# Linear attention in a two-layer decoder kernel: VectorE's feature map of the first step moves ahead of measuring the next batch, TensorE's turning of the next rows behind two other turnings

## The reference, cut to what matters

```python
def _phi(x):
    return jax.nn.elu(x) + 1.0
qkv = jnp.einsum('bld,ed->ble', x, w_qkv)
q, k, v = (_phi(qkv[0]), _phi(qkv[1]), qkv[2])
def step(carry, inp):
    S = S + k_t[..., :, None] * v_t[..., None, :]
    z = z + k_t
    num = jnp.einsum('bhde,bhd->bhe', S, q_t)
    den = jnp.maximum(jnp.sum(z * q_t, axis=-1, keepdims=True), EPS)
    return ((S, z), num / den)
return jnp.einsum('bld,ed->ble', out, w_out)
```

## Time and profile before

| | |
|---|---|
| median of three runs | 3820.56 us |
| profiled execution, its own time | 3820.83 us |
| its span | 3819.1 us |
| TensorE busy (matmul) | 3505.7 us, 92% |
| VectorE busy | 2801.9 us, 73% |
| ScalarE busy | 2065.1 us, 54% |
| GpSimd busy | 395.4 us, 10% |
| mean granted TensorE clock | 0.971 of full speed |

### The profile page before, as it was taken

The page is one execution under the profiler, slowest core; times in us unless marked ns, Lnnn a source line. Parts: engine busy times, 40 slices in busy tenths (PEclk is TensorE's granted clock), DMA queues, the critical chain, the costliest instruction groups (busy, mean ns, idle before and its releaser), DMA issues. The chain is left out here.

```text
span 3819.1 us, 91322 instructions
## 1 busy us (share of the span) xinstructions
PE 3505.7 (92%) x28322; PEld 2917.3 (76%) x28322; DVE 2801.9 (73%) x8965; ACT 2065.1 (54%) x6485; POOL 395.4 (10%) x582
## 2 busy tenths in 40 slices
PE   6999999899999999339968889999799999999999
PEld 5888888688888888239956656676588888888887
DVE  5666666677777776646658877888788878788786
ACT  5777777677777776325545548888432223222232
POOL 0000000000000000341168302222000000000000
PEclk9999999999999999669989999999899999999999
DMA  3000000010000000542211000000200000000000
GB/s 101 1 0 0 0 0 0 18 51 11 11 11 13 14 11 1 175 137 77 78 55 45 15 17 20 22 22 17 87 26 11 14 8 16 8 11 14 8 14 9
DMA packets 56108, 109.69 MB, mean 29 GB/s; under 512 B 8368, under 2 KB 27184, under 8 KB 55728
## 3 DMA queue, kind: packets, MB, share of 16 engines
q1 hardware_dynamic: 46656, 80.72, 6.7%
q0 software_dynamic: 8464, 26.22, 2.1%
q10 hardware_dynamic: 864, 1.19, 0.1%
HBM read 72.46 MB, written 35.65 MB: 28 GB/s over the span
## 5 line engine op out<-in xcount | busy, mean ns | idle before, releaser
L2255 DVE TENSOR_TENSOR f_zgT<-f_zT,f_ps_g 128x512 fp32r<-128x512 f32 x512 | 327.3, 681 | 14.0 <-PE f_ps_g L2086 9.9
L639 ACT ACTIVATE c_pr<-c_sm,c_nmx 128x256 f32<-128x256 f32 x512 | 254.5, 498 | 147.7 <-DVE c_nmx L485 147.7
L127 PE MATMUL f_ps_out<-f_out_rounded,f_zgT 128*128 128x256 f32 x1024 | 295.3, 288 | 0.0
L128 PE MATMUL f_ps_out<-f_out_rest,f_zgT 128*128 128x256 f32 x1024 | 289.5, 283 | 0.0
L2208 DVE TENSOR_TENSOR f_gv<-f_ps_v,f_gm 128x512 f32<-128x512 f32 x256 | 175.6, 686 | 154.2 <-PE f_ps_v L129 154.1
L129 PE MATMUL f_ps_out<-f_out_rounded,f_zgT 128*128 128x256 f32 x1024 | 288.0, 281 | 0.0
L639 ACT ACTIVATE a_pr<-a_sm,a_nmx 128x128 f32<-128x128 f32 (+1 forms) x512 | 227.1, 445 | 98.1 <-DVE a_nmx L485 98.1
L485 DVE CUSTOM_DVE_ANT_0 a_sm<-a_ps_s,causal 128x128 f32<-128x128 f32 (+1 forms) x512 | 152.5, 354 | 156.8 <-PE a_ps_s L371 156.7
L485 DVE CUSTOM_DVE_ANT_0 c_sm<-c_ps_s,c_mask 128x256 f32<-128x256 f32 x512 | 186.7, 420 | 87.1 <-PE c_ps_s L371 86.7
L127 PE MATMUL f_ps_v<-f_val_rounded,f_xs 128*128 128x512 f32 x512 | 214.8, 419 | 6.7 <-DVE f_gv L2208 6.7
L2337 ACT ACTIVATE f_pr<-f_sm,f_nmx 128x128 f32<-128x128 f32 (+1 forms) x256 | 115.0, 450 | 185.5 <-DVE f_nmx L2228 185.5
(11 more groups left out here) (384 smaller groups left out, 11231.8 us busy)
## 6 DMA issues: line engine op xcount, KB each, us to landing
f_slot_rows<-f_run POOLq DMA_DIRECT2D x1, 9216.0 KB, 34.8
f_rows<-f_slot_rows SPq DMA_DIRECT2D x72, 128.0 KB, 2.0
f_slot_out<-f_y SPq DMA_DIRECT2D x72, 128.0 KB, 1.9
c_ctx_stage<-in_ctxT SPq DMA_DIRECT2D x32, 256.0 KB, 2.8
small<-in_f_w SPq DMA_DIRECT2D x16, 512.0 KB, 3.9
x_sb<-in_x SPq DMA_DIRECT2D x8, 512.0 KB, 8.3
small<-in_c_w SPq DMA_DIRECT2D x8, 512.0 KB, 4.0
c_mask_stage<-in_mask SPq DMA_DIRECT2D x16, 256.0 KB, 3.0
```

The lines of the kernel that those rows point to most:

```text
L127: nc.tensor.matmul(out, sh, mh, start=start, stop=False, **kw)
L128: nc.tensor.matmul(out, sh, ml, start=False, stop=False, **kw)
L639: last = nc.scalar.activation(pr[:, r, i, 0:n], sm[:, j, i, 0:n], ACT.Exp, bias=nmx[:, j, i:i + 1], scale=-1.0, accum_out=sums[:, r, i:i + 1])
L2255: last = nc.vector.tensor_tensor(zgT[:, k % 2, r], zT[:, s % 2, r, :].bitcast(F32).unsqueeze(1).broadcast_to([P, 2, S]), ps_g[:].rearrange ...
```

## The change

TensorE: in the linear attention only, `turn_x` moves in step 3 from the head of the slot to behind `back` and `turn_o`. VectorE: `features` of step 0 moves ahead of the first masking and of `measure`, which itself moves from ahead of `finish` to behind `features`; `features` of step 2 keeps its place, between the first and second masking. In the last batch, which measures nothing, `features` of step 0 still moves ahead of the first masking.

```diff
@@ TensorE
             def slot(b, s):
-                if s == STEPS - 1 and (not isinstance(b, int) or b + 1 < B):
+                if softmax and s == STEPS - 1 and (not isinstance(b, int) or b + 1 < B):
                     turn_x(b + 1)
                 if at := lagged(b, s, 0, STEPS):
                     project(*at)
...
                     turn_o(at[2])
+                if not softmax and s == STEPS - 1 and (not isinstance(b, int) or b + 1 < B):
+                    turn_x(b + 1)
                 two = lagged(b, s, 2, STEPS) if softmax else None
@@ VectorE
                 else:
-                    if s == 0 and (not isinstance(b, int) or b + 1 < B):
-                        measure(b + 1)
                     if ended:
                         finish(*ended)
                     for j in range(J):
+                        if now and s % 2 == 0 and j == s // 2:
+                            features(*now)
+                            if s == 0 and (not isinstance(b, int) or b + 1 < B):
+                                measure(b + 1)
                         if one:
                             keep_past(one[0], one[1], j)
-                        if now and s % 2 == 0 and j == 0:
-                            features(*now)
                     if one:
                         fill_v(*one)
```

## The result

The changed kernel takes 3806.72 us, the median of five runs (3804.79 to 3811.46), against 3820.56 for the kernel before. The ratio is 0.9962 (95% interval 0.9951 to 0.9973): 13.8 us less, where 10.3 were forecast, and inside the range. The profiled execution took 3811.46 us, the longest of the five, for a span of 3809.7 at a mean granted clock of 0.968.

A forecast was written before the change was run, and what follows sets the result against it. The prediction took the linear attention's order of work to bound it: VectorE waits for z's turning back, behind a late feature map. 9.2 us from waits plus 1.1 from batch 0 made 10.3 less, 3810.3 us, range 3804.5 to 3816.5.

The forecast's parts named there:

- The ring: Linear attention batch: feature map, v projection, turning back of z (L1511), finish; VectorE's 9.4 us in 14 waits stem from it.
- Part 1: Step 0's feature map ahead of measuring and first masking: 0.70 us per undisturbed batch, 9.2 us over the stage.
- Part 2: Measuring placed after the feature map in step 0: costs nothing, covered by ScalarE's earlier start.
- Part 3: turn_x behind back and turn_o in step 3: others fill its 0.44 us stall; no gain, no loss.
- Part 4: Batch 0's feature map, 1.8 us late, starts earlier but partly at the lower clock: 1.1 us, between 0 and 1.8.
- Part 5: Last batch, without measuring, waits 1.49 us for the turning back behind the output matmuls: no gain.
- Part 6: Gap of 0.64 us at the loop's top, 12 times: taken as nothing, bounds -1.4 and +1.2 us.
- Beside GpSimd: Disturbed part of the stage, before 2133: 5.1 us for eight waits, mostly as long as undisturbed ones.
- A: GpSimd takes the gain in disturbed batches; six undisturbed ones and batch 0 leave 5.3 us, 3815.3. Chance 0.12.
- B: Gap at the loop's top was measuring's; up to 0.61 us goes 12 times, 7.3 us more, 3803.0. Chance 0.08.
- C: ScalarE's table loads and v copy come 0.3 us later, delaying TensorE's projection: 4 us given back, 3814.3. Chance 0.07.
- D: TensorE's full clock granted one batch later after batch 0: some +15 us against -10, 3825. Chance 0.03.

The follow-up runs named there:

- e6: The change, with step 3's statistics of the finished batch moved between finish and the four maskings: 3840.18 us, ratio 0.999, undisturbed batch 17.62 us.
- e3: The changed kernel with measuring left at the head of step 0, ahead of finish: ratio 1.0005 to the kernel before, undisturbed batch 17.97 us.
- e4: The change with step 0 as finish, measuring, first masking, feature map: ratio 1.0004 to the kernel before, undisturbed batch 18.37 us.
- e1: Kernel before with only turn_x moved, VectorE's order as before: 3848.59 us against 3844.66, ratio 1.0007, undisturbed batch 18.44 us.
- b2: Changed kernel with turn_x in its old place (VectorE's part alone), last job: 3807.89 us against 3822.41, ratio 0.9963, undisturbed batch 17.50 us.
- e2b: VectorE's part of the change alone, turn_x in its old place, run again in the second job: 3837.75 us, ratio 0.9982 to the kernel before.
- b1: The change itself, run again in the last job: 3808.97 us against 3822.41 for the kernel before, ratio 0.9967.
- b7: VectorE's part alone, plus step 3's statistics of the finished batch ahead of the fill, last job: 3805.57 us against 3822.41, ratio 0.9957.
- a1: The change itself, run again in the second job: 3840.99 us against 3844.88 for the kernel before, ratio 0.9991.
- e2: Changed kernel with turn_x in its old place (VectorE's part alone), first run: 3840.12 us against 3844.66, ratio 0.9981, undisturbed batch 17.50 us.
- e5: The change, with step 3's statistics of the finished batch ahead of the fill copies: 3839.11 us, ratio 0.9985 to the kernel before.

## Why the prediction was right, and where its terms were not

The forecast was 3810.3 us with a range of 3804.5 to 3816.5; measured, 3806.72. The ring that it named is the one that bounded the batch: the wait for L1511 that it set out to remove went, and e6 brought it back. That the total is off by only 3.6 us owes something to luck, as the ledger below shows: two terms too large stand against two gains that it didn't have. Its parts, in its order:

- **Part 1, the feature map.** Right in place and nearly in size. It put 0.70 us on the stretch up to step 1's first masking (5.73 us from the batch's start); measured 0.62 (5.81 us). What it said would be late next is what is late next: maskings end at 2203.70 + 1.95 = 2205.65, the next one starts 1.07 us later, against the 1.06 that was taken over from step 3, with 0.17 us of waiting for the scores. The 9.2 us over the stage took the list's whole waits; at 0.62 us in each of 13 batches they would be 8.1.
- **Part 2, measuring.** Nothing lost, as forecast: ScalarE's table load starts 3.06 us behind the batch's first instruction, instead of 2216.14 - 2212.22 = 3.92. But the part was costed by itself, and e3 and e4 show that it can't be: without it the feature map is worth 0.47 us, with it 0.95.
- **Part 3, turn_x.** Right. e1 has the batch of before to 0.01 us, and b2 has the gain without it. In the change step 3 reads

```profile
2211.96 0.44 PE L1511 MATMUL l_ps_t<-ident,l_zT 128*128 128x128 f32 x2 [0.49 <-ACT l_zT L1800]
2212.24 0.60 PE L1521 MATMUL l_ps_t<-ident,l_o_all 128*128 128x128 f32 x4
2212.68 0.60 PE L1428 MATMUL l_ps_p<-ident,l_xn 128*128 128x128 f32 x4
...
2213.62 0.94 PE L1472 MATMUL l_ps_s<-l_qk,l_split 32*128 32x256 f32 x16 [0.34 <-DVE l_wT L1636]
```

  and the scores still wait for the maskings, 0.34 us instead of 0.17. The others did not fill the stall, as the prediction had it: `back` at the head waits 0.49 us for ScalarE's copy of z, where turn_x waited 0.44 us for the feature map. The maskings end last either way, and so nothing came of it in an undisturbed batch; beside ScalarE's stand a loss of some 3 us is not excluded (e1, e2b).
- **Part 4, batch 0.** Forecast 1.1 us, bounds 0 to 1.8. The feature map came at once behind its input (1968.06 + 0.63, then 1968.72), and the maskings of step 1 stand 1.5 us earlier from the stage's start. Little is left at batch 1:

```profile
1976.73 0.82 DVE L1614 COPY l_vp<-l_v_all 128x64 f32<-128x64 f32 x2
...
1985.05 0.17 DVE L1642 TENSOR_SCALAR l_den<-l_ps_t 128x8 f32<-128x8 f32 x1 [0.83 <-PE l_ps_t L1511]
```

  The fill took 0.82 us beside GpSimd instead of 0.38, and `finish`, now first in line, waits 0.83 us where measuring used to fill that time. Batch 1 starts 40.16 us behind the stage's start instead of 40.27, and 39.80 in b1. The term, 0.1 and 0.5 us, lies near its lower bound.
- **Part 5, the last batch.** Right: 1.50 us of waiting where there were 1.49.
- **Part 6, the top of the loop.** The failed term: taken as nothing, measured 0.31 us a batch, 12 times, 3.7 us, outside its bounds of -1.4 to +1.2 (in this profile 10 of the 12 starts show the gap of some 0.33 us, two show none). It is why the undisturbed batch is 17.49 us and not the 17.7 to 17.8 that was named as the sign. Its reason, "two register instructions fewer", was too small by far, and the row that said so was quoted beside it: outside the loop `finish` followed the statistics with no gap. Here a gap that the profile puts down to "issue" at a loop's top belonged in half to the instruction behind it.
- **Beside GpSimd.** Forecast, 5.1 us for eight waits, of which 4.3 us in six lie in batches 2 to 8; measured, 9.5 us in these seven batches (7.4 in b1). Seven times the 0.95 us of an undisturbed batch is 6.7, which leaves 2.8 (0.7 in b1). VectorE is also busy 3.1 us less in them (121.9 before, 118.8 with the change; b1 1.3 less), 1.6 of it in the fill's copies (0.1 in b1), so that meetings with GpSimd cost less, by an amount that differs from execution to execution. The sum of the waits was no upper bound. (The fill of 1.02 us in the earlier trace rows stands in batch 4, the one batch in the loop without the wait, as counted here.)

The ledger for the profile: forecast 9.2 + 1.1 = 10.3; measured in the stage 12.7, of which the loop's top gave 3.7, the batches beside GpSimd 2.8 more than undisturbed ones, and batch 0 0.1, with 1.6 lost to the clock at the end. That leaves 7.7 us for the waits, where 9.2 were forecast.

**The rivals.** A, GpSimd takes the gain, is refuted where ScalarE doesn't stand, and with the opposite sign: a disturbed batch gained 1.35 us (1.05 in b1), an undisturbed one 0.95. In the two jobs where ScalarE does stand the total came out near A's (3.9 us of gain, A had 5.3), but by a wait of ScalarE. The rule of the Trainium skill that was set beside it (SBUF — State Buffer, Who interferes with whom), that the engine that issues first holds the shared port pair for its whole instruction and the other blocks, agrees with pairs of copies that took 0.82 us beside 0.28; the step from it, that the delays stay with the number of GpSimd's instructions, fell: that number was the same, and b7's copies took 275 ns on the mean where b1's took 354. B, the gap was measuring's, was half right: 0.31 of its 0.61 us went, and it shortened the batch only together with the other move (e4 has the shorter gap and 0.07 us of gain). C, ScalarE's chain, didn't come: the copy of v at 2206.99 lets TensorE start the projection at 2207.61 without a wait. D, the clock: counted from the stage's start, full speed came in batch 0 within 0.5 us of the time at which it came before. It fell again at the end of the stage, which D had no place for, at 1.6 us.

## What to carry to other kernels

An engine's order within a slot is worth reading as a ring: find the wait that ends last, name the instruction ahead of it whose input had long been ready, and move that one ahead; the next limit can be forecast from a step that is already in that state. The gains of two moves need not add up: here one gave 0.47 us, the other 0.07, both 0.95, so test them apart and together. Where an instruction with more waits and register work ahead of it goes, behind the loop's top, a short instruction or a long one, is worth a run of its own. And a gain can shrink to a third in another job, if an engine stands there for reasons of its own; compare the undisturbed batch first, then the total.

## What was not expected of the hardware

- ScalarE's stand of 3.1 to 4.1 us (a1, 2000:2120) once in each round of GpSimd's four gathers, in two jobs and not in the other runs, with nothing in the profile that releases it. The stage of the same kernel is 28.5 us longer in the job that has it (a1: 351.1 us, b1: 322.6). The granted clock shows it too: 0.93 and 0.83 in a1's 2040:2090 and 2090:2130, where the first profiles have 1.00. What holds ScalarE stays open.
- TensorE's clock drops from 2.4 to 1.2 GHz in the stage's tail in one execution and not in another of the same kernel (e2 against b2: 1.99 and 3.78 us for the same eight matmuls), with nothing in the program that differs.
- The 0.64 us at the loop's top, against the compare-and-branch of about 108 ns that the Trainium skill states (Advanced Engine Details and Errata, Control Flow Timing): no run here shows the branch by itself, but at least 0.31 us of the gap were not its, and with e5, where 0.23 us are left, 0.41.
